# The last piece of x in 13 transfers of 16 down to 2 rows, each with its own semaphore

## What is computed

```
emb  = x @ factors                      # x is 1024 x 12500, factors 12500 x 16
reg  = x @ W_lin.T + b_lin
sumsq = square(emb.sum(axis=1))
sqsum = (square(x) @ square(factors)).sum(axis=1)
h    = relu(emb @ W1.T + b1)            # 16 -> 128
h    = relu(h @ W2.T + b2)              # 128 -> 64
dnn  = h @ W3.T + b3                    # 64 -> 1
out  = 0.5 + 5 * sigmoid(reg + 0.5 * (sumsq - sqsum) + dnn)
```

## Time and profile before

| | |
|---|---|
| median of 3 runs | 134.65 us (134.56 to 134.65) |
| the profiled execution's own time | 134.6 us |
| its span, first to last instruction | 132.4 us |
| PE, DVE, ACT, POOL busy | 81%, 40%, 48%, 9% of the span |
| granted TensorE clock, mean | 0.997 of full speed |
| HBM read | 52.22 MB, 394 GB/s over the span |

### The profile page before, as it was taken

How to read it: one execution, slowest core, us unless ns; L and a number is a source line. 1 busy time by engine, 2 the same in 40 slices (tenths; PEclk the granted TensorE clock), 3 DMA queues, 4 the chain that set the end, 5 groups by cost and what they waited for, 6 DMA issues and landing times.

```text
span 132.4 us, 2859 instructions
## 1 busy us (share of the span) xinstructions
PE 106.6 (81%) x1123; PEld 31.6 (24%) x1123; DVE 53.1 (40%) x51; ACT 64.1 (48%) x72; POOL 12.5 (9%) x48
## 2 busy tenths in 40 slices
PE   6089999768877877877978869996967966989992
PEld 4012222111111211211212312211111111335881
DVE  0392450532531541540540292450451351576571
ACT  4031660734733743742744394652662562465851
POOL 4016001110010011011011001151000000000000
PEclk9999999999999999999999999999999999999998
DMA  4999999999999999999999999999999999999800
GB/s 115 397 460 431 430 431 426 430 426 431 421 435 426 435 426 416 440 426 431 431 426 426 426 430 426 421 440 416 435 421 431 435 418 424 411 411 411 321 13 6
DMA packets 4639, 52.34 MB, mean 395 GB/s; under 512 B 532, under 2 KB 664, under 8 KB 1688
## 3 DMA queue, kind: packets, MB, share of 16 engines
q1 hardware_dynamic: 4632, 52.23, 93.6%
HBM read 52.22 MB, written 0.00 MB: 394 GB/s over the span
## 4 chain that ended last, share of the span: by engine, by line
DMA 63%; PE 28%; SPq 3%; ACT 3%; issue 2%; DVE 1%; ACTq 0%
DMA xr<-in_x_groups 52%; PE p_lin L467 22%; DMA xr<-in_x_end 11%; ACT sq L298 2%; PE p_sq L467 2%; PE p_h L557 2%; SPq L236 1%; PE p_tot L467 1%; PE p_h L588 1%; DVE h L419 0%; DVE h L414 0%; PE p_tot L570 0%; SPq L234 0%; SPq L233 0%; SPq L232 0%
## 5 line engine op out<-in xcount | busy, mean ns | idle before, releaser
L298 ACT ACTIVATE sq<-xr 128x1536 f32<-128x1536 f32 (+1 forms) x40 | 48.5, 1262 | 47.2 <-DMA xr<-in_x_groups 47.2
L394 DVE TENSOR_TENSOR sq<-xr 128x1536 f32<-128x1536 f32 x20 | 35.1, 1758 | 56.6 <-DMA xr<-in_x_groups 56.6
L467 PE MATMUL p_lin<-xr,wr 128*17 128x512 f32 x320 | 38.2, 594 | 13.8 <-DMA xr<-in_x_groups 13.8
L467 PE MATMUL p_lin<-sq,wz 128*18 128x512 f32 x320 | 38.2, 594 | 2.3 <-ACT sq L298 1.0
L467 PEld LDWEIGHTS p_lin<-xr,wr 128*17 128x17 f32 x320 | 7.9, 97 | 42.3 <-issue 21.6
L467 PEld LDWEIGHTS p_lin<-sq,wz 128*18 128x18 f32 x320 | 8.2, 97 | 31.5 <-ACT sq L298 16.9
L273 POOL COPY wr<-hd x20 | 7.4, 372 | 71.5 <-PE p_lin L467 70.8
L402 DVE TENSOR_TENSOR sq<-xr 128x320 f32<-128x320 f32 (+5 forms) x15 | 10.4, 724 | 8.1 <-DMA xr<-in_x_end 8.1
L307 ACT ACTIVATE sq<-xr 128x320 f32<-128x320 f32 (+5 forms) x15 | 9.1, 652 | 7.1 <-DMA xr<-in_x_end 7.1
L467 PE MATMUL p_lin<-xr,hd 128*17 128x352 f32 (+1 forms) x128 | 10.0, 380 | 1.5 <-DMA xr<-in_x_end 1.5
L467 PE MATMUL p_lin<-sq,ws 128*18 128x352 f32 x64 | 6.6, 459 | 0.0
(11 more groups left out here) (50 smaller groups left out, 34.7 us busy)
## 6 DMA issues: line engine op xcount, KB each, us to landing
xr<-in_x_groups SPq DMA_DIRECT2D x20, 2048.0 KB, 15.4
xr<-in_x_end SPq DMA_DIRECT2D x1, 2112.0 KB, 10.8
xr<-in_x_end SPq DMA_DIRECT2D x3, 640.0 KB, 12.3
xr<-in_x_end SPq DMA_DIRECT2D x1, 1760.0 KB, 14.6
xr<-in_x_end SPq DMA_DIRECT2D x1, 1056.0 KB, 12.7
hd<-in_head SPq DMA_DIRECT2D x1, 952.0 KB, 4.8
xr<-in_x_end SPq DMA_DIRECT2D x1, 704.0 KB, 14.1
xf<-in_x_first SPq DMA_DIRECT2D x1, 512.0 KB, 5.7
```

The lines of the kernel that those rows point to most:

```text
L298: nc.scalar.activation(sq[:, s, c:c + n, :], xr[:, s, c:c + n, :], ACT.Square).then_inc(act_squared, 1)
L394: nc.vector.tensor_tensor(sq[:, s, 0:BY_DVE, :], xr[:, s, 0:BY_DVE, :], xr[:, s, 0:BY_DVE, :], ALU.mult).then_inc(dve_squared, 1)
L467: return nc.tensor.matmul(out, lhsT, rhs, start=False, stop=False, skip_group_check=True)
```

## The change

The transfer of piece 8 becomes 13 transfers, of 16, 15, 14, 13, 12, 11, 10, 9, 8, 7, 6, 5 and 2 rows (128 together). Each raises a semaphore of its own (`last_landed[j]`), and PE, ACT and DVE each wait for all 13 where they waited for `end_landed[8]`. Bytes, addresses, squares and matmuls stay as they are.

```diff
+STAIRS = (16, 15, 14, 13, 12, 11, 10, 9, 8, 7, 6, 5, 2)
+assert sum(STAIRS) == P
...
-        end_landed = [sem(f"end_landed{i}") for i in range(len(PIECES))]
+        end_landed = [sem(f"end_landed{i}") for i in range(len(PIECES) - 1)]
+        last_landed = [sem(f"last_landed{j}") for j in range(len(STAIRS))]
...
+        def piece_landed(engine, i):
+            if i < len(PIECES) - 1:
+                engine.wait_ge(end_landed[i], 16)
+            else:
+                for j in range(len(STAIRS)):
+                    engine.wait_ge(last_landed[j], 16)
...
                 sp.wait_ge(sq_used, TOTAL + last_slot(i) + 1)
-                sp.dma_start(piece(xe, i, c, n), rows).then_inc(end_landed[i], 16)
+                if i < len(PIECES) - 1:
+                    sp.dma_start(piece(xe, i, c, n), rows).then_inc(end_landed[i], 16)
+                else:
+                    p = 0
+                    for j, k in enumerate(STAIRS):
+                        sp.dma_start(piece(xe, i, c, n)[p:p + k, :], rows[p:p + k, :]).then_inc(last_landed[j], 16)
+                        p += k
...
                 if j == 0:
-                    act.wait_ge(end_landed[i], 16)
+                    piece_landed(act, i)
...
                 if j == 0:
-                    dve.wait_ge(end_landed[i], 16)
+                    piece_landed(dve, i)
...
-                pe.wait_ge(end_landed[i], 16)
+                piece_landed(pe, i)
```

## The result

The changed kernel takes 136.37 us in the median of 4 runs (135.78 to 136.75), against 134.62 us for the kernel before, measured beside it (134.56 to 134.65). The ratio is 1.0126, 95% interval 1.0081 to 1.0172: slower by 1.75 us, more than the noise and above the range of the prediction (134.5 to 135.6). A second set of runs of the same kernel gave 1.0154 (1.014 to 1.0168).

What follows compares the result with a forecast made beforehand. It took PE's unbroken work after the x stream to bound the end. Waits on PE cost 0.15 us, issue and the waits on DVE and ACT 0, an earlier landing nothing: 134.65 + 0.15 = 134.8 us, range 134.5 to 135.6.

Steps and rivals of the forecast that it cites:

- What bounds the kernel: End of the kernel: PE works without a break from 116.28 to 129.03; piece 8 lands 0.1 to 0.2 us before PE needs it.
- Why piece 8 lands late: DMA engines at piece 8: four go on 0.7 us longer than the others; guessed cause, six 16 KB instruction loads.
- Step 1: Piece 8's transfers: k rows use the k lowest-numbered engines, one row each; 13 rows on engines 0 and 1, 1 on engine 15.
- Step 2: Cost on a DMA engine: 0.048 us a row, plus 0 to 0.09 us per extra semaphore write, taken as 0.03.
- Step 3: Piece 8's landing: if the late engines have 4 rows or fewer, about 0.1 us earlier than 126.85, worth nothing to PE.
- Step 4: SP's issues of piece 8: thirteen in place of one, over between 118.4 and 121.4, cost 0 with 3 us of cover.
- Step 5: Waits for piece 8: six events and one carried wait each on PE, ACT and DVE; 0.15 us on PE, 0 elsewhere.
- The lowest engines become the late ones: Rival at piece 8's landing: low engines, or late ones in the middle, land at 127.3; +0.5 us, about 135.15 us; 20%.
- The rival of transfers worked off one after another: Rival on the DMA queue: 13 small transfers in turn at 1.0 us each, 12 us more, 146 us; 5%.
- The signs to look for: Changed kernel's profile: what would show the forecast right (first matmul of piece 8 near 127.1) or wrong (PE gap over 0.3 us).

Runs made afterwards that it cites:

- the experiment with the waits alone: Kernel before with piece 8 still one transfer, but PE, ACT and DVE each also waiting for 12 semaphores raised long ago; 134.75 us against 134.73, ratio 1.0004.

## Why the prediction was wrong, by its steps

- **What bounds the kernel** was right: PE's order after 116.28, a margin of 0.1 us or less in front of piece 8, and a delay of piece 8 that goes to the end. PE's start on it moved by 2.44 us, the span by 2.6 us and the own time of the profiled execution by 2.15 us.
- **Why piece 8 lands late** was right in its number, four engines, and in that an earlier landing is worth nothing. That the instruction loads make them late was a guess, and the traces speak for it. In the kernel before, loads of 16 KB start at 19.85, 77.85, 93.17 and 121.11 and take 1.02 to 1.07 us each, and the transfers that land at 23.74, 82.48, 97.17 and 123.70 are the first with one, two, three and four late engines. All twelve profiles show these steps; in the second profile of the kernel before, the first load starts at 23.88 and the first late landing is at 28.38. No run took the loads away, so the cause is not shown.
- **Step 1, engines and rows**, was right: 4744 packets, one row for each engine.
- **Step 2, "I take 0.03, near the row with the same 1280-byte rows"** failed. This is the mis-sized term. A further transfer on an engine costs 0.17 to 0.20 us where it brings one row, against 0.048 + 0.03 = 0.08 us in the sum, and 0.14 us even at my upper bound. The bounds came from gaps between pieces of 8 rows an engine, where the completion runs beside the data and can't be seen. A bound taken from a place where a cost is hidden is no bound; the final store, with SP's last wait of 1.0 us for it, was the row nearest to an uncovered completion, and it should have been the upper end.
- **Step 3, "if the four late engines are those with 4 rows or fewer"** failed too. They are 5, 6, 9 and 10, with 11, 10, 7 and 6 transfers. Engine 5 ends 11 completions behind piece 7: 11 x 0.2 = 2.2 us, where the whole piece had taken 0.40. Had the late engines been those with 4 rows or fewer, as step 3 has it, then at 0.2 us a completion both they, with 4 of them, and the low engines, with 13, would have ended near 127.6 (an estimate from 126.81 + 4 x 0.2, and from the 127.63 of the last transfer), not at 129.05.
- **Step 4, issue**, was right: free, and over at 117.8, a little before the 118.4 of its lower bound.
- **Step 5, the waits**: six events on each engine was right. An event on PE is 0.1 us in a row of them, not 0.06. The prediction took the waits in the order of the source, with four events behind the last late landing; they stand in another order, and three follow it, from the fourth on, 0.35 us in the profile. (Its sum 126.85 + 0.24 + 0.04 is 127.13, not 127.15, which changes nothing.) In the time they cost nothing measurable by themselves: at most 0.19 us, by the interval of the experiment with the waits alone.
- **The rivals.** "The lowest engines become the late ones" named the mechanism in its second half, late engines in the middle, but priced what an engine with 11 rows adds at 0.44 us where it was 1.8 us (2.24 - 0.40). The rival of transfers worked off one after another held the right idea, that completions don't overlap each other, but put all 13 on one line at 1.0 us each; they are in turn only on their own engine, and 0.2 us each. The Trainium skill (DMA: Bandwidth & Descriptors, "Anatomy of one DMA") says of transfers issued by GpSimd that the semaphore can't be raised before the last byte is confirmed in the target memory, and gives a fixed part of some 2 us for each. The transfers here are issued by SP. That a completion comes after the data the trace shows too (126.89 against 126.44 in the kernel before), but each further one costs 0.2 us here, not 2.
- **The signs to look for**: "a gap of PE over 0.3 us behind piece 7" was what came, and the other sign, a DMA share above 0.1 after 126.5, was not: it is 0.08 and then 0.00. That sign looked for late data; late completions don't show in the share. PE's first matmul of piece 8 is at 129.40 and the first layer at 130.34, where the prediction had 127.1 and 128.0 to 128.1.

## What to carry to other kernels

Count transfers for each DMA engine, not only bytes: where a transfer gives an engine less than about 0.2 us of data (here under 4 rows of 1280 bytes), the completion is what it costs, in turn with the others of that engine. Of the seven ways to cut the last transfer tried here none was faster than the whole one. Whoever wants to cut by rows to balance engines should first find out which engines are late, from the landings by engine. A price read between large transfers says nothing of small ones.

## What the runs showed of the hardware that was not expected

- Completions of one engine come 0.17 to 0.20 us apart when each transfer brings it a row or two of 1280 bytes, though the trace has such a row at 0.055 us; two over 4 rows each take 0.35 us in all, no more than one over 8 rows (0.40 us).
- After the last data (126.82) the completions went on until 129.05, and the DMA share read 0.00 in the last 2 us.
- The four late engines were 5, 6, 9 and 10 in both profiles of the changed kernel. They landed piece 7 at 126.62 to 126.81, the last of the others at 125.65.
- The number of late engines grew by one with each of four 16 KB instruction loads, in all twelve profiles.
- Thirteen waits written in the order of the transfers were not carried out in it: the first event held those for 10 and 9 rows, the last those for 15 and 2.
- A wait instruction on PE carries two conditions and takes 51 ns, but in a row they come 0.1 us apart; on DVE too, on ACT 0.08 us.
- Cutting piece 8 makes piece 7, issued before it, land 0.2 to 0.5 us later on the late engines.
